# The causal mask of layer 1's attention, moved from selects on the probabilities to matmuls on the scores

## Chip, core and metric

The kernel runs on one core of a Trainium2 chip. The metric is the device time of one execution in microseconds, median of three runs. Engines are named as in the profile: PE (matmuls), PEld (PE's weight loads), DVE, ACT, POOL, and SP, which issues DMAs.

## What is computed

Two transformer layers with a layer norm after each of their four blocks, on x of shape (4, 512, 256). Layer 0 is a grouped-query attention without a mask and a mixture of eight experts. Layer 1, which the change touches, is a causal attention with 16 heads of 16 and a feed-forward block of width 1024:

```python
qkv = x @ W_qkv.T + b_qkv
scores = einsum('bnqd,bnkd->bnqk', q, k) * 0.25
scores = where(triu(ones((S, S)), k=1), -inf, scores)   # key after query
attn = softmax(scores)
out = einsum('bnqk,bnkd->bnqd', attn, v)
y = layernorm(x + out @ W_out.T + b_out)
```

## The kernel before

All code is one program with semaphores written by hand. Each engine walks the same written list of steps, `c_steps` for layer 1, and does its own part of each. The lists are strings (C_START to C_END, lines 82 to 98), so the order on every engine is fixed; an engine that waits holds up all that stands behind it on that engine.

Layer 1's attention goes over 4 batches, 4 groups of 4 heads and 4 key tiles of 128: 64 steps, 16 in a batch. Step k has two parts:

- `cattS` k: PE computes the scores of four heads, transposed (keys on partitions, queries along the row), one PSUM bank each, columns from `P * kt` to 512, so 512, 384, 256 or 128 columns as kt goes from 0 to 3 (L847). Only the first 128 of them, the diagonal block, need a mask. The row maxima have been put into the product as two more rows of q and k, so ACT only takes the exponential (L1003), two heads per instruction. PE signals `s_full` after each pair of heads, ACT `exp_done` after each pair.
- `cattP` k: PE multiplies the probabilities by V and a column of ones (L860), four heads side by side in the 32-column groups of the array.

Between the two stands POOL: after both exponentials it zeroes, with one `affine_select` over the diagonal blocks of four heads (128x512), the probabilities whose key comes after the query (L1436), and signals `masked`. PE waits for `masked` ahead of `cattP` (L858).

`attention_order` (line 119) interleaves: `cattS` k+1, then the fills of step k, then `cattP` k. The fills are the other work of the layer: for the next batch the projections (cX, cQ, cK, cV), the row maxima (m) and the packing of the maxima (cM); for the batch before the normalisation of the heads (cF, cG), the output projection with its layer norm (cP, cN) and the feed-forward (cH, cD). A fill of kind m is a unit of 512 columns: PE computes scores (L824) and adds the causal mask to the diagonal block by a matmul of the identity with `negmask` (L826), DVE reduces it to maxima (L1335). Units go through three PSUM banks in a ring (`take`, `filled`, `consumed`); `negmask` is -1e30 above the diagonal, in bf16. L599 is the helper of all PE transposes, L607 that of all other products of the fills. L1049 to L1070 are DVE's layer norm, L1309 to L1311 its split of q and k into bf16 parts (cK), L993 is ACT's part of cQ and waits for the store of parts two units back; L1007 evacuates the attention output.

POOL's other work in this stage is the gather of layer 0's expert rows for the next batch (L1414), issued when DVE has finished with the batch before. Layer 0's attention has the same two parts (`attS` L641, `attP` L655) with no mask: `attP` waits for `exp_done` of the first pair at its first head and for that of the second pair at its third.

Of the kernel before, what the change touches and what calls it, by code (L numbers as in the profile page):

```python
# [25 lines left out]
ALU = mybir.AluOpType  # L26
# [3 lines left out]
P = 128  # L30
B = 4
# [3 lines left out]
NT = S // P  # L35
# [115 lines left out]
def post_ln_layers(nc, ins, out):  # L151
# [4 lines left out]
    with ExitStack() as ctx:  # L156
# [101 lines left out]
        base = place([E])  # L258
# [104 lines left out]
        s_stack2 = [sem(f"last_q_stacks_loaded{i}") for i in range(2)]  # L363
        s_full = [sem(f"scores_full{i}") for i in range(2)]
        exp_done = [sem(f"exp_done{i}") for i in range(2)]
        masked = sem("probs_masked")
        pv_done = sem("pv_done")
        o_evac = sem("o_evacuated")
        x1_ready = sem("x1_ready")
# [223 lines left out]
        def _(pe):  # L593
# [185 lines left out]
            for step in c_steps:  # L779
# [5 lines left out]
                elif n == "Wb":  # L785
                    transposes(step, [(0, n_b[0:4 + NK, :], ident[0:4 + NK, 0:4 + NK], P)])
                elif n == "Wu":
                    pe.wait_ge(deq, 1)
                    c, half = i // 2, i % 2
                    transposes(step, [(P * r, n_up[:, 4 * half + r, cols(c)], ident, P) for r in range(4)])  # L790
                elif n == "Wul":
                    c, half = i // 2, i % 2
                    consumed(pe, ("Wat", 0, 0))
                    products(step, [((P, 0, 512), [(ua_t[0:RANK, cols(c)], n_ub[0:RANK, 512 * half:512 * half + 512])])])
                elif n == "Wd":
                    pe.wait_ge(deq, 2)
                    transposes(step, [(P * (2 * r + c), n_dn[:, c, cols(2 * i + r)], ident, P)
                                for r in range(2) for c in range(2)])
                elif n == "Wdl":
                    consumed(pe, ("Wat", 0, 2))  # L800
                    products(step, [((P, C * r, C * (r + 1)), [(da_t[0:RANK, cols(2 * i + r)], n_db[0:RANK, :])])
                                    for r in range(2)])
                elif n in ("cX", "cN"):
                    pe.wait_ge(x2_ready if n == "cX" else x3_ready, 2 * b + i + 1)
                    transposes(step, [(P * (2 * t + c), x_sb[:, NT * b + 2 * i + t, cols(c)], ident, P)
                                for t in range(2) for c in range(2)])
                elif n == "cQ":
                    consumed(pe, ("cX", b, 0))
                    consumed(pe, ("cX", b, 1))
                    w_cols = cols(2 * (i % 2) + i // 2)  # L810
                    products(step, [((P, 0, S), [(w1_qkv[:, c, w_cols], c_x_t[:, c, :]) for c in range(2)])])
                elif n == "cV":
                    products(step, [((P, C * t, C * (t + 1)),
                                     [(c_x_t[:, c, cols(2 * i + t)], w1_qkv[:, c, 2 * C:3 * C]) for c in range(2)])
                                    for t in range(2)])
                elif n == "max":

                    qt, h0, nh = MAXES[i]
                    if i % (len(MAXES) // 2) == 0:
                        pe.wait_ge(cs_stack[h0 // (NH // 2)][b % 2], 32 * (b // 2 + 1))  # L820
                    dst = take(pe, step)
                    w = P * (qt + 1)
                    for g in range(nh):
                        nc.tensor.matmul(dst[:, w * g:w * (g + 1)], cq_stack[0:STACK, b % 2, h0 + g, cols(qt)],  # L824
                                         ck_stack[0:STACK, b % 2, h0 + g, 0:w], start=True, stop=True)
                        last = nc.tensor.matmul(dst[:, w * g + P * qt:w * (g + 1)], identb, negmask,  # L826
                                                start=False, stop=True, skip_group_check=True)
                    last.then_inc(full_of(step), 1)
                elif n == "cM":
                    pe.wait_ge(m_parts, b + 1)  # L830
                    dst = take(pe, step).bitcast(BF16)
                    for t in range(NT):
                        last = nc.tensor.transpose(dst[0:2 * NH, cols(t)], mparts[:, t, :, :].rearrange("p a h -> p (a h)"),
                                                   identb)
                    last.then_inc(full_of(step), 1)
                elif n == "cattS":
                    hg, kt = i // NT, i % NT
                    k = head0 * B + headc * b + i
                    if i == 0:
                        pe.wait_ge(s_m, 32 * (b + 1))  # L840
                        pe.wait_ge(kones, 1)
                    for g in range(4):
                        h = 4 * hg + g
                        if g % 2 == 0:

                            pe.wait_ge(exp_done[g // 2], k)
                        last = nc.tensor.matmul(ps[:, g, P * kt:S], ck_stack[0:STACK + 2, b % 2, h, cols(kt)],  # L847
                                                cq_stack[0:STACK + 2, b % 2, h, P * kt:S], start=True, stop=True)
                        if g % 2:
                            last.then_inc(s_full[g // 2], 1)  # L850
                elif n == "cattP":
                    hg, kt = i // NT, i % NT
                    if i == 0:
                        consumed(pe, ("cV", b, 0))
                        consumed(pe, ("cV", b, 1))
                    if kt == 0:
                        pe.wait_ge(o_evac, HG * (B + b) + hg)
                    pe.wait_ge(masked, headc * b + i + 1)  # L858
                    for g in range(4):
                        last = nc.tensor.matmul(ps[32 * g:32 * g + 32, 4, P * kt:S],  # L860
                                                cv_aug[:, b % 2, kt, 4 * hg + g, :],
                                                cprobs[:, i % 2, g, P * kt:S], start=(kt == 0), stop=(kt == NT - 1))
                    last.then_inc(pv_done, 1)
                elif n == "cF":
                    pe.wait_ge(o_evac, HG * (B + b + 1))
                    transposes(step, [(P * hg, co_sb[:, hg, cols(i)], ident, P) for hg in range(HG)])
                elif n == "cG":
                    consumed(pe, ("cF", b, 2 * i))
                    consumed(pe, ("cF", b, 2 * i + 1))
                    transposes(step, [(P * (2 * t + c), cattn[:, t, cols(c)], ident, P)  # L870
                                for t in range(2) for c in range(2)])
                elif n == "cP":
                    consumed(pe, ("cG", b, i))
                    products(step, [((P, C * t, C * (t + 1)),
                                     [(c_a_t[:, c, cols(2 * i + t)], w1_o[:, c, :]) for c in range(2)])
                                    for t in range(2)])
                elif n == "cH":
                    consumed(pe, ("cN", b, 0))
                    consumed(pe, ("cN", b, 1))
                    products(step, [((P, 0, S), [(w_up[:, c, cols(i)], c_x3_t[:, c, :]) for c in range(2)])])  # L880
                elif n == "cI":

                    half, k = i // NK, i % NK
                    consumed(pe, ("cN", b, half))
                    tok = slice(C * half, C * half + C)
                    products(step, [((P, 0, C), [(w_up[:, c, cols(k)], c_x3_t[:, c, tok]) for c in range(2)])])
                elif n == "cD":
                    for k in range(NK):
                        consumed(pe, ("cI", b, NK * (i // 2) + k) if ("cI", b, 0) in unit_no else ("cH", b, k))
                    products(step, [((P, 0, C), [(hid_t[:, k, cols(i)], w_dn[:, k, :]) for k in range(NK)])])  # L890
# [485 lines left out]
        def _(pool):  # L1376
# [47 lines left out]
            for step in c_steps:  # L1424
                n, b, i = step
                if n == "cL" and i == 1 and b + 1 < B:
                    pool.wait_ge(x2_ready, 2 * b + 2)
                    gather(b + 1)
                elif n == "cattS":

                    k = head0 * B + headc * b + i
                    kt = i % NT
                    pool.wait_ge(exp_done[0], k + 1)
                    pool.wait_ge(exp_done[1], k + 1)
                    diag = cprobs[:, i % 2, :, P * kt:P * (kt + 1)]
                    nc.gpsimd.affine_select(out=diag, in_=diag, compare_op=ALU.is_ge, fill=0.0, base=0,  # L1436
                                            pattern=[[0, 4], [1, P]], channel_multiplier=-1).then_inc(masked, 1)


_NAMES = {  # L1440
# [53 lines left out]
```

## Time and profile before

| | before |
|---|---|
| median of 3 runs | 959.66 us (957.38 to 961.69) |
| the profiled execution, own time | 959.16 us |
| its span, first to last instruction | 957.4 us |
| granted TensorE clock, mean | 0.921 |
| PE busy | 815.9 us (85%), 4084 instructions |
| DVE busy | 466.6 us (49%) |
| ACT busy | 372.8 us (39%) |
| POOL busy | 131.3 us (14%), 129 instructions |

Layer 1's attention fills the stretch from 600 to 906 us of the span. The granted clock has two values in this trace, 1.00 (2.4 GHz) and 0.50 (1.2 GHz), so a mean between them tells how much of a stretch ran at either. PE's busy time counts a matmul to its modelled end, and matmuls overlap: the true interval of a matmul in a stream is the distance from its start to the next start.

### The profile page before, as it was taken

What the parts mean: (1) busy time and instruction counts of PE and PEld (TensorE: products, weight loads), DVE (VectorE), ACT (ScalarE), POOL (GpSimd) and SP (SyncE); (2) the same over time, 40 slices, a digit from 0 to 9 for tenths busy, and PEclk for the clock granted to TensorE, in tenths of its full rate; (3) what the DMA queues carried; (4) which work ended last, traced back from release to release, by engine and by line L of the source; (5) the groups of instructions that cost most, each with busy time, mean ns of one, the idle gap of its engine ahead of it and who ended that gap; (6) DMA issues with size and microseconds to landing.
All of it is one profiled execution on the core that took longest, in us unless ns stands there. A gap on an engine that the chain in (4) does not pass through costs nothing. (4 is left out here: it accounts for less than half of the span.)

```text
span 957.4 us, 12102 instructions
## 1 busy us (share of the span) xinstructions
PE 815.9 (85%) x4084; PEld 438.9 (46%) x4085; DVE 466.6 (49%) x1317; ACT 372.8 (39%) x591; POOL 131.3 (14%) x129
## 2 busy tenths in 40 slices
PE   4598999999998649999983687979798979979986
PEld 3223435444345336666642334435354544543675
DVE  3721741751436222222246877587745675553263
ACT  3387685875742001111121121644332533246230
POOL 0000000000000611111665010213010100112000
PEclk8699999999999979999975787989899979999989
DMA  6558116025060051111110854002800180000000
GB/s 191 112 168 173 60 61 130 0 64 83 23 219 23 1 162 45 46 47 44 33 55 22 253 161 136 2 2 65 222 1 2 34 253 1 2 1 23 12 12 22
DMA packets 55259, 71.01 MB, mean 74 GB/s; under 512 B 8678, under 2 KB 49592, under 8 KB 53672
## 3 DMA queue, kind: packets, MB, share of 16 engines
q1 hardware_dynamic: 52824, 65.22, 24.8%
q0 software_dynamic: 2384, 5.12, 2.0%
q8 instruction: 30, 0.49, 0.2%
q14 instruction: 21, 0.17, 0.1%
HBM read 46.45 MB, written 23.74 MB: 73 GB/s over the span
## 5 line engine op out<-in xcount | busy, mean ns | idle before, releaser
L607 PE MATMUL ps<-arena 128*128 128x256 f32 (+5 forms) x1084 | 335.6, 459 | 16.2 <-ACT arena L980 4.3
L607 PEld LDWEIGHTS ps<-arena 128*128 128x128 f32 (+1 forms) x1084 | 203.8, 198 | 107.4 <-issue 67.7
L922 ACT ACTIVATE arena<-ps 128x1024 f32<-128x1024 f32 x128 | 124.0, 1026 | 40.8 <-PE ps L641 40.7
L599 PE MATMUL ps<-arena 128*128 128x128 f32 (+4 forms) x430 | 71.6, 311 | 74.5 <-DVE arena L1070 32.2
L1335 DVE TENSOR_REDUCE arena<-ps 128x1 f32<-128x512 f32 (+3 forms) x176 | 101.2, 636 | 43.4 <-PE ps L826 42.6
L1003 ACT ACTIVATE arena<-ps 128x1024 f32<-128x1024 f32 (+3 forms) x128 | 83.3, 705 | 86.4 <-PE ps L847 86.1
L599 PEld LDWEIGHTS ps<-arena 128*128 128x128 f32 (+4 forms) x430 | 56.4, 158 | 97.2 <-DVE arena L1070 36.0
L722 PE MATMUL ps<-arena 128*128 x184 | 86.6, 593 | 1.2 <-DVE arena L1239 1.2
L1436 POOL TENSOR_SCALAR_AFFINE_SELECT arena<-arena 128x512 f32<-128x512 f32 x64 | 43.2, 675 | 288.2 <-ACT arena L1003 288.1
L641 PE MATMUL ps<-arena 96*128 96x512 bf16 x256 | 71.9, 394 | 12.6 <-DMA arena<-parts_dram 9.8
L824 PE MATMUL ps<-arena 96*128 96x128 bf16 (+3 forms) x256 | 65.5, 315 | 11.6 <-DVE arena L1335 7.0
L655 PE MATMUL ps<-arena 128*32 128x512 f32 x512 | 70.2, 616 | 0.0
L947 ACT ACTIVATE arena<-ps 128x512 f32<-128x512 f32 x23 | 13.8, 598 | 143.0 <-PE ps L722 143.0
L847 PE MATMUL ps<-arena 98*128 98x512 bf16 (+3 forms) x256 | 50.1, 316 | 11.3 <-ACT arena L1003 8.2
L1382 POOL DMA_INDIRECT id_dram<-arena x16 | 15.7, 979 | 316.1 <-DVE arena L1221 311.5
L641 PEld LDWEIGHTS ps<-arena 96*128 96x128 bf16 x256 | 18.4, 98 | 88.4 <-ACT arena L922 34.6
L826 PE MATMUL ps<-arena 128*128 128x128 bf16 x256 | 50.6, 227 | 0.0
L860 PE MATMUL ps<-arena 128*32 128x128 f32 (+3 forms) x512 | 48.9, 454 | 0.0
L824 PEld LDWEIGHTS ps<-arena 96*128 96x128 bf16 x256 | 25.5, 100 | 43.7 <-DVE arena L1335 27.4
L722 PEld LDWEIGHTS ps<-arena 128*128 128x128 f32 x184 | 33.1, 190 | 25.3 <-issue 24.2
L739 PE MATMUL ps<-arena 128*128 x184 | 43.6, 380 | 0.8 <-ACT arena L953 0.8
L847 PEld LDWEIGHTS ps<-arena 98*128 98x128 bf16 x256 | 18.5, 99 | 55.8 <-issue 31.0
(135 smaller groups left out, 757.0 us busy)
## 6 DMA issues: line engine op xcount, KB each, us to landing
arena<-stacks_dram SPq DMA_DIRECT2D x16, 768.0 KB, 6.6
arena<-in_gate_up_proj SPq DMA_DIRECT2D x8, 1024.0 KB, 8.8
arena<-parts_dram SPq DMA_DIRECT2D x48, 128.0 KB, 4.3
stacks_dram<-arena SPq DMA_DIRECT2D x16, 384.0 KB, 3.0
arena<-in_down_proj SPq DMA_DIRECT2D x8, 512.0 KB, 9.3
stacks_dram<-arena SPq DMA_DIRECT2D x16, 256.0 KB, 3.2
parts_dram<-arena SPq DMA_DIRECT2D x8, 384.0 KB, 4.2
yg_dram<-arena SPq DMA_DIRECT2D x23, 128.0 KB, 1.7
```

Of the source, the lines that this page charges most:

```text
L599: last = nc.tensor.transpose(dst[0:rows, col:col + n], src, idn)
L607: last = nc.tensor.matmul(dst[0:rows, lo:hi], a, w, start=(n == 0), stop=(n == len(pairs) - 1))
L641: last = nc.tensor.matmul(ps[:, g, :], k_stack[0:STACK, b % 2, hg, cols(kt)], q_stack[0:STACK, b % 2, 4 * hg + g, :], start=True, stop=True)
L655: last = nc.tensor.matmul(ps[32 * g:32 * g + 32, 4, :], v_aug[:, kt, hg, :], (probs0, probs1)[i % 2][:, g, :], start=(kt == 0), stop=(kt = ...
L722: last = nc.tensor.matmul(ps[:, 2 * half + up, :], xg_t[:, half, c, :], gu[:, e, c, FE * up:FE * (up + 1)], start=(c == 0), stop=(c == 1))
L824: nc.tensor.matmul(dst[:, w * g:w * (g + 1)], cq_stack[0:STACK, b % 2, h0 + g, cols(qt)], ck_stack[0:STACK, b % 2, h0 + g, 0:w], start=Tru ...
L826: last = nc.tensor.matmul(dst[:, w * g + P * qt:w * (g + 1)], identb, negmask, start=False, stop=True, skip_group_check=True)
L847: last = nc.tensor.matmul(ps[:, g, P * kt:S], ck_stack[0:STACK + 2, b % 2, h, cols(kt)], cq_stack[0:STACK + 2, b % 2, h, P * kt:S], start= ...
L860: last = nc.tensor.matmul(ps[32 * g:32 * g + 32, 4, P * kt:S], cv_aug[:, b % 2, kt, 4 * hg + g, :], cprobs[:, i % 2, g, P * kt:S], start=( ...
L922: nc.scalar.activation(probs[:, 2 * p:2 * p + 2, :], ps[:, 2 * p:2 * p + 2, :], ACT.Exp)\
L1003: nc.scalar.activation(cprobs[:, i % 2, 2 * p:2 * p + 2, P * kt:S], ps[:, 2 * p:2 * p + 2, P * kt:S], ACT.Exp).then_inc(exp_done[p], 1)
L1335: nc.vector.tensor_reduce(mneg[:, qt, h0:h0 + nh], filled(v, step)[:, 0:nh * w].rearrange("p (h n) -> p h n", n=w), AX.X, ALU.max, negate= ...
```

## The change

Each `cattS` issues four more matmuls, two after each pair of score matmuls: `negmask` as the stationary operand and the identity as the moving one, so that -1e30 is added to the scores whose key comes after the query, in the diagonal 128 columns of each head's bank. They stand ahead of the signal `s_full`. POOL's 64 selects and their semaphore go, and `cattP` waits for ACT's `exp_done`, the first pair ahead of its first head and the second pair ahead of its third.

```diff
--- before.py
+++ after.py
@@ -363,7 +363,6 @@
-        masked = sem("probs_masked")
@@ -847,6 +846,9 @@
                         last = nc.tensor.matmul(ps[:, g, P * kt:S], ck_stack[0:STACK + 2, b % 2, h, cols(kt)],
                                                 cq_stack[0:STACK + 2, b % 2, h, P * kt:S], start=True, stop=True)
                         if g % 2:
+                            for d in (g - 1, g):
+                                last = nc.tensor.matmul(ps[:, d, cols(kt)], negmask, identb, start=False, stop=True,
+                                                        skip_group_check=True)
                             last.then_inc(s_full[g // 2], 1)
@@ -855,8 +857,9 @@
                     if kt == 0:
                         pe.wait_ge(o_evac, HG * (B + b) + hg)
-                    pe.wait_ge(masked, headc * b + i + 1)
                     for g in range(4):
+                        if g % 2 == 0:
+                            pe.wait_ge(exp_done[g // 2], head0 * B + headc * b + i + 1)
                         last = nc.tensor.matmul(ps[32 * g:32 * g + 32, 4, P * kt:S],
@@ -1426,15 +1429,6 @@
                 if n == "cL" and i == 1 and b + 1 < B:
                     pool.wait_ge(x2_ready, 2 * b + 2)
                     gather(b + 1)
-                elif n == "cattS":
-
-                    k = head0 * B + headc * b + i
-                    kt = i % NT
-                    pool.wait_ge(exp_done[0], k + 1)
-                    pool.wait_ge(exp_done[1], k + 1)
-                    diag = cprobs[:, i % 2, :, P * kt:P * (kt + 1)]
-                    nc.gpsimd.affine_select(out=diag, in_=diag, compare_op=ALU.is_ge, fill=0.0, base=0,
-                                            pattern=[[0, 4], [1, P]], channel_multiplier=-1).then_inc(masked, 1)
```

## Rows read from the trace of the kernel before

**Rows 1.** The page: busy time, share of the span and instructions of each engine.

```profile
PE 815.9 (85%) x4084; PEld 438.9 (46%) x4085; DVE 466.6 (49%) x1317; ACT 372.8 (39%) x591; POOL 131.3 (14%) x129
```

**Rows 2.** Busy us by engine, count, granted clock: attention's end; a half-clock stretch.

```profile
864.00:905.70 41.70, 41.23 (x224) 22.19 (x222) 11.40 (x45) 18.79 (x31) 6.84 (x10) 0.99 0.06 20
639.20:646.00 6.80, 5.40 (x24) 2.69 (x25) 6.11 (x28) 3.84 (x5) 0.64 (x1) 0.50 0.01 3
```

**Rows 3.** Who waited for whom, 560 to 957 us: total, times, longest.

```profile
POOL arena L1436 <- ACT arena L1003: 288.1, 60, 43.1
...
PEld ps L860 <- issue: 23.3, 59, 0.8
...
PEld ps L860 <- POOL arena L1436: 1.5, 2, 0.8
```

**Rows 4.** Timeline around the P parts of steps 25 and 1: start, duration, engine.

```profile
697.04 0.63 POOL L1436 TENSOR_SCALAR_AFFINE_SELECT arena<-arena 128x512 f32<-128x512 f32 x1 [8.29 <-ACT arena L1003]
...
705.36 0.22 PE L826 MATMUL ps<-arena 128*128 128x128 bf16 x1
...
705.50 0.16 PEld L860 LDWEIGHTS ps<-arena 128*32 128x32 f32 x8 [0.27 <-issue]
...
600.95 0.64 POOL L1436 TENSOR_SCALAR_AFFINE_SELECT arena<-arena 128x512 f32<-128x512 f32 x1 [0.76 <-ACT arena L1003]
...
601.37 0.61 PE L847 MATMUL ps<-arena 98*128 98x256 bf16 x4
...
601.90 0.16 PEld L860 LDWEIGHTS ps<-arena 128*32 128x32 f32 x8 [0.21 <-issue]
```

**Rows 5.** Timeline: a P part and what follows it, layer 0 and layer 1.

```profile
150.97 1.06 PE L655 MATMUL ps<-arena 128*32 128x512 f32 x8
151.97 1.04 PE L641 MATMUL ps<-arena 96*128 96x512 bf16 x4
...
600.37 1.07 PE L860 MATMUL ps<-arena 128*32 128x512 f32 x8
```

**Rows 6.** Timeline of PE: first and last of eight matmuls of 128 columns.

```profile
599.81 0.22 PE L824 MATMUL ps<-arena 96*128 96x128 bf16 x1
...
600.22 0.22 PE L826 MATMUL ps<-arena 128*128 128x128 bf16 x1
```

**Rows 7.** Timeline: stalls of PE and ACT, with idle time before and releaser.

```profile
636.81 0.34 PE L833 MATMUL ps<-arena 128*32 128x128 bf16 x3 [0.82 <-DVE arena L1343]
...
640.60 1.89 PE L847 MATMUL ps<-arena 98*128 98x512 bf16 x4 [2.96 <-DMA arena<-arena]
...
672.64 1.26 ACT L993 ACTIVATE arena<-ps,arena 128x512 f32<-128x512 f32 x2 [6.32 <-DMA stacks_dram<-arena]
...
674.45 0.29 PE L847 MATMUL ps<-arena 98*128 98x128 bf16 x2 [2.71 <-ACT arena L1003]
...
743.08 0.50 PE L847 MATMUL ps<-arena 98*128 98x384 bf16 x2 [0.42 <-ACT arena L1003]
...
860.89 1.12 PE L599 MATMUL ps<-arena 128*128 128x128 f32 x4 [4.18 <-DVE arena L1070]
```

**Rows 8.** Waits of PE for cV on DVE, 640 to 700 us.

```profile
PE ps L599 <- DVE arena L1321: 1.3, 1, 1.3
```

**Rows 9.** Timeline: DVE operations beside a select of POOL, and the same without.

```profile
655.13 0.64 POOL L1436 TENSOR_SCALAR_AFFINE_SELECT arena<-arena 128x512 f32<-128x512 f32 x1 [2.22 <-ACT arena L1003]
...
655.21 0.83 DVE L1310 CAST arena<-arena 128x512 bf16<-128x512 f32 x1
...
669.42 0.43 DVE L1310 CAST arena<-arena 128x512 bf16<-128x512 f32 x1
...
853.43 0.16 DVE L1068 SCALAR_TENSOR_TENSOR arena<-arena 128x2 f32<-128x2 f32 x1
...
854.01 0.64 DVE L1068 SCALAR_TENSOR_TENSOR arena<-arena 128x2 f32<-128x2 f32 x1
```

**Rows 10.** Groups of DVE instructions, 600 to 906 us: count, busy us, mean ns.

```profile
L1310 DVE CAST arena<-arena 128x512 bf16<-128x512 f32 x8 | 5.2, 645 | 0.3
```

## The prediction

> **What bounds the kernel now.** I read the page first. PE is busy for 85% of the span, every other engine for less than half [rows 1], so work added to PE is suspect and work taken from POOL is not yet a gain. Then the table by stage. In the last 42 us of layer 1's attention PE is busy 41.23 of 41.70 us [rows 2]: nothing there can hide PE work. Then the waits. POOL's selects wait 288 us for ACT, so POOL is idle nearly all the time, and PE's weight loads of the P part wait for POOL only twice, 1.5 us in all [rows 3]. Last the timeline of single steps, to see whether even that is real. In step 25 the select starts at 697.04 and the P part at 705.50: it was ready 7.8 us early, because the fills stand between S k+1 and P k. The P part starts 0.14 us after the last matmul ahead of it. The tightest case is step 1, which has no fills: the select ends at 601.59 (600.95 + 0.64); the four score matmuls of 256 columns start at 601.37 and last to 601.98 by the model, and the weights of P load at 601.90, as they do elsewhere just ahead of the running matmul's modelled end [rows 4]. So POOL holds PE up nowhere that I can find. What ends the attention stage is PE's own stream, broken by a few waits for DVE, ACT and DMA at the seams of the batches [rows 7].
>
> **The change, part by part.**
>
> *Four matmuls per S part.* 4 x 64 = 256 matmuls of 128 columns in bf16, each with its own weight load. The maxima have the same kind: score and mask matmuls by turns, new weights each time. Eight of them start from 599.81 to 600.22, so 0.41/7 = 0.0586 us each at the full clock; the weight loads are hidden [rows 6]. 256 x 0.0586 = 15.0 us. The steps whose S part lies at the half clock pay double. I count two, steps 16 and 17: at 640.60 four score matmuls of 512 columns take 1.89 us [rows 7] in a stretch whose granted clock is 0.50, the lower level of 1.2 GHz [rows 2]. That is 8 x 0.0586 = 0.5 us more. Sum 15.5 us, 0.234 us for each S part.
>
> The Trainium skill, TensorE: Matmul & The Clock Gate, section Back-to-back issue gap, speaks against the change more strongly: it gives about 81 ns for a 128-column matmul in a stream of weight loads and matmuls. By that figure the four mask matmuls would cost an estimated 20.7 us instead of 15.0. The rows at hand measure the very pattern, so the sum goes by them.
>
> *What of it is covered.* An added matmul costs nothing where PE then waits for something whose start does not depend on it. I walked the 64 steps:
> - Ahead of the packing of maxima PE waits 0.82 us for DVE L1343, which hangs on the last max unit, issued earlier [rows 7]. The S part in between is covered, in three batches: 0.7 us.
> - In batches 1 and 2 ACT sits 6.32 us on the DMA of the q and k parts, then PE 2.71 us on ACT, and then 1.3 us on DVE's cV [rows 7, 8]. Two S parts ahead of the stall and one inside it are covered, twice: 6 x 0.234 = 1.4 us.
> - In the last batch PE waits 4.18 us for a layer norm [rows 7]; two S parts lie in the shadow of that chain: 0.5 us.
> - Where the fills are few, PE waits inside the S part for the exponentials of the step before, as the 0.42 us at 743.08 [rows 7]. There the first pair's masks are covered, some seven times, 0.12 to 0.23 us each: 1.3 us.
> - The first steps of batches 1 and 2 wait in the chain of transposes and head normalisation: 0.6 us.
>
> Together 4.5 us. In the bursts of maxima PE also waits for DVE in a ring, but DVE itself idles at each seam between two bursts while PE does P and S, so a later PE makes DVE later too: I count no cover there. Nor in steps 53 to 63 [rows 2]. If none of this cover held, the cost would be 15.5; if the rings covered too (about 16 more steps), 11.0 - 3.7 = 7.3.
>
> *s_full comes later* by 0.12 us for each pair, and ACT's exponentials with it. P k stands behind S k+1, which already waits for the exponentials of k, so no new wait arises in P; in the steps without fills the delay is that of the fourth point.
>
> *The wait of P.* It moves from `masked` to two `exp_done`. Both are met when S k+1 has started. Saving: nothing with fills between; at most the 1.5 us of [rows 3]. I take 0. Cost of the second wait: layer 0's P part has it and lasts 1.00 us from its start to the next S part (150.97 to 151.97), the same as layer 1's (600.37 to 601.37) [rows 5, 4]. I take 0.
>
> *64 selects go.* POOL is idle otherwise; what stands behind them in its queue, the gather for a later batch, is needed many steps later. Gain 0 on POOL, but not on DVE: the CAST of cK at 655.21, beside a select, took 0.83 us, the same at 669.42 took 0.43; an operation of the layer norm at 854.01 took 0.64 against 0.16 [rows 9]. Eleven DVE operations are stretched so, by 3.8 us in all, operation by operation; nearly half of that is CAST, whose mean of 0.645 over eight is 0.217 above 0.43 [rows 10]. Most lies where PE does not wait. On a chain that PE waits for I find 0.31 and 0.37 us in batch 1, 0.31, 0.31 and 0.31 in batch 2 and 0.48 in batch 3: 2.1 us gained. Bounds: 0 and 3.8. The Trainium skill, SBUF — State Buffer, section Who interferes with whom, says that a DVE instruction with two SBUF inputs and a GpSimd instruction that reads SBUF exclude each other. Its whole promise is this term, and the trace agrees for 854.01.
>
> **The sum.** 15.5 - 4.5 - 2.1 = +8.9 us on the profiled execution's 959.16 (span 957.4 and 1.8 around it): 968.1. The median of the runs is 0.5 higher, so I forecast 968.5 us.
>
> **The rivals.** About 0.5% (4.8 us) is what a measurement of this kernel can tell from no change.
>
> *Full price.* The cover is not there, or more S parts fall to the lower clock: a stall that moves can bring another stretch like that of 639.2 to 646.0 [rows 2], in which 6.8 us do the work of 3.4. Then 15.5 - 0 to 2, plus 3.4: +13 to +19, about 975. For it: PE is the bound nearly throughout. Against: the stalls of [rows 7] are real idle time. By the skill's 81 ns the sum would be an estimated 5.7 us above the forecast, in this rival's range. Chance 0.17.
>
> *Nearly hidden.* The rings cover (7.3 us left, as above), and DVE gains its full 3.8: +3.5, about 963. A low-clock stretch that vanishes because the stalls ahead of it shrink brings it near, 8.9 - 3.4 = +5.5. Against: DVE idles at the seams. Chance 0.15.
>
> *Faster.* The handoff over POOL is the wait after all. Its place is the idle time ahead of L860's weight loads, 23.3 us over 59 steps, which the profile puts down to "issue" [rows 3]; a semaphore that arrives late could hide in it. Removed, the sum is 8.9 - 23.3 = -14.4, about 945; the change wins from the point at which over 8.9 us of it are POOL's. Against: in step 25 the select was long done and the 0.27 us were there still [rows 4]. Chance 0.06.
>
> **The numbers.** Forecast 0.62, full price 0.17, nearly hidden 0.15, faster 0.06. Slower by over 0.5%: the first two, less a tail of the forecast, 0.77. Within 0.5%: 0.17. Faster: 0.06. The range runs from 962.0, which takes in part of the nearly hidden case, to 975.5, all cover gone (959.66 + 15.5 = 975.2).
>
> **What would show it.** Right: no row L1436; 256 more matmuls that start 0.058 us apart within L847's groups; P parts still 0.14 us behind the matmul ahead; steps 53 to 63 longer by 2.6 us (11 x 0.234); the waits of 4.18 and 2.71 us shorter by about 0.5 each; CAST back at 0.43. Wrong: P parts that follow faster than before (POOL was the wait), mask matmuls at over 0.07 us, or other low-clock stretches than before.

## The result and the profile after

| | before | after |
|---|---|---|
| median, first series | 959.38 us (4 runs) | 972.22 us (4 runs) |
| ratio, 95% interval | | 1.0128 [1.0111, 1.0146] |
| profiled execution, own time | 959.16 us | 973.52 us |
| its span | 957.4 us | 971.7 us |
| first S part | 596.38 us | 602.28 us |
| last P part | 904.80 us | 922.14 us |

The changed kernel is slower, by 12.8 us in this series. It was run in two more series, beside the kernel before: 1.0086 [1.0064, 1.0107] and 1.0091 [1.0060, 1.0122] (below). So the change costs 8 to 12 us by the three ratios, 6 to 14 with their intervals; the forecast was +8.9. Two executions of later series that took far longer, 4387 us of the kernel before and 1647 us of the one with the masks ahead of the scores, are in no ratio.

The page of the changed kernel, busy time by engine, answers to [rows 1]:

```profile
PE 832.3 (86%) x4340; PEld 454.9 (47%) x4341; DVE 464.1 (48%) x1317; ACT 374.3 (39%) x591; POOL 88.2 (9%) x65
```

PE has 256 instructions more, POOL 64 fewer. POOL lost 43 us of work and DVE 2.5 us, PE gained 16.4.

The attention stage by itself, from the first S part to the last P part, and its end, from the P part of step 53 to that of step 63; first the kernel before, then the changed one (columns as in [rows 2]):

```profile
596.38:904.80 308.42, 274.46 (x1669) 145.66 (x1668) 180.96 (x498) 126.46 (x202) 46.94 (x68) 0.95 0.17 48
868.08:904.80 36.72, 36.72 (x205) 20.27 (x204) 7.34 (x27) 16.61 (x27) 6.20 (x9) 1.00 0.05 16
```

```profile
602.28:922.14 319.86, 290.59 (x1925) 162.11 (x1924) 177.22 (x498) 127.81 (x202) 3.79 (x4) 0.95 0.16 46
883.04:922.14 39.10, 39.10 (x241) 22.32 (x240) 6.32 (x23) 16.62 (x27) 0.00 (x0) 1.00 0.04 15
```

The stage grew by 11.4 us. Its end, where PE never idles in either kernel, grew by 2.38 us with 36 matmuls more: nine S parts at 0.26 us.

The other 2.9 us of the two spans' difference lie outside the attention stage, where the code of both kernels is the same. Ahead of the attention the changed kernel's profile lies 5.9 us back, behind it 3.0 us forward. The same window of the expert stage, untouched by the change, first before, then after (the granted clock is the third number from the end):

```profile
290.00:390.00 100.00, 75.97 (x287) 48.39 (x285) 30.83 (x91) 13.47 (x22) 25.15 (x26) 0.91 0.21 59
```

```profile
290.00:390.00 100.00, 75.16 (x263) 46.90 (x262) 29.86 (x95) 12.38 (x20) 24.25 (x25) 0.85 0.19 55
```

One ran at 0.91, the other at 0.85, and got 24 matmuls less done. In further profiles of the two kernels the first S part stood at 598.2 (before), 597.9 and 599.2 us (after): most of the 5.9 us is the chance of one execution. What follows the last P part took 52.6 and 49.6 us in two profiles of the kernel before, 49.6, 49.6 and 51.1 in three of the changed one.

Now the S part in steps 24 to 26 of the changed kernel, from PE's timeline; the P part is L863, the scores L846, the masks L850:

```profile
712.58 0.22 PE L825 MATMUL ps<-arena 128*128 128x128 bf16 x1
...
712.73 1.06 PE L863 MATMUL ps<-arena 128*32 128x512 f32 x8
713.73 0.39 PE L846 MATMUL ps<-arena 98*128 98x256 bf16 x2
713.96 0.28 PE L850 MATMUL ps<-arena 128*128 128x128 bf16 x2
714.07 0.38 PE L846 MATMUL ps<-arena 98*128 98x256 bf16 x2
714.29 0.28 PE L850 MATMUL ps<-arena 128*128 128x128 bf16 x2
714.41 0.33 PE L823 MATMUL ps<-arena 96*128 96x384 bf16 x1
...
715.07 0.22 PE L825 MATMUL ps<-arena 128*128 128x128 bf16 x1
715.22 0.16 PEld L863 LDWEIGHTS ps<-arena 128*32 128x32 f32 x8 [0.27 <-ACT arena L1006]
```

A pair of masks goes from 713.96 to 714.07, 0.11 us; over whole intervals (below) four of them cost 0.23 us, 0.057 a matmul. The P part of step 25 still loads its weights 0.15 us after the last fill (715.07 to 715.22) with the same 0.27 us of idle time ahead of it as in [rows 4]. Over all steps those idle times, 23.3 us in [rows 3], are what they were:

```profile
PEld ps L863 <- issue: 23.1, 57, 1.0
```

The 1.5 us that [rows 3] puts down to POOL are now 0.3 us put down to ACT. They had held up no P part: at both places, 653.08 and 804.27, PE was busy with matmuls of a fill up to its start.

And DVE's CAST of cK, [rows 10], is at its undisturbed time:

```profile
L1313 DVE CAST arena<-arena 128x512 bf16<-128x512 f32 x8 | 3.4, 426 | 0.3
```

The most telling comparison is one that the rows allow without a model: how much longer is the interval from each P part to the next than it was before? Interval k runs from P k-1 to P k and holds the S part of step k+1. Of 63 intervals, 29 grew by 0.22 or 0.23 us, 17 by 0.28, eleven by no more than 0.11 or not at all, and six moved otherwise (the interval in brackets): -1.35 (22), -0.68 (38), -0.76 (52), +0.42 (15), +0.97 (47), +1.10 (53).

### The profile page after: what moved, and what is told of

The parts are those of the page before. It is cut to its first block and busy times, and to the rows that moved or that the text cites. A ratio compares the mean times of both kernels' runs of the same rounds, so it can differ in the third digit from the quotient of the medians.

```text
span 971.7 us, 12485 instructions
## 1 busy us (share of the span) xinstructions
PE 832.3 (86%) x4340; PEld 454.9 (47%) x4341; DVE 464.1 (48%) x1317; ACT 374.3 (39%) x591; POOL 88.2 (9%) x65
## 5 line engine op out<-in xcount | busy, mean ns | idle before, releaser
L598 PE MATMUL ps<-arena 128*128 128x128 f32 (+4 forms) x430 | 69.6, 305 | 73.6 <-DVE arena L1073 32.2
L1338 DVE TENSOR_REDUCE arena<-ps 128x1 f32<-128x512 f32 (+3 forms) x176 | 101.2, 634 | 50.2 <-PE ps L825 49.6
L721 PE MATMUL ps<-arena 128*128 x184 | 89.4, 611 | 1.2 <-DVE arena L1242 1.2
L640 PE MATMUL ps<-arena 96*128 96x512 bf16 x256 | 71.9, 394 | 12.3 <-DMA arena<-parts_dram 9.5
L846 PE MATMUL ps<-arena 98*128 98x512 bf16 (+3 forms) x256 | 56.5, 313 | 10.0 <-ACT arena L1006 6.2
L863 PE MATMUL ps<-arena 128*32 128x128 f32 (+3 forms) x512 | 48.9, 454 | 0.0
L721 PEld LDWEIGHTS ps<-arena 128*128 128x128 f32 x184 | 34.2, 196 | 27.1 <-issue 26.0
L738 PE MATMUL ps<-arena 128*128 x184 | 43.6, 380 | 0.8 <-ACT arena L956 0.8
L738 PEld LDWEIGHTS ps<-arena 128*128 128x128 f32 x184 | 34.9, 190 | 15.1 <-issue 11.6
L1367 DVE TENSOR_TENSOR arena<-ps,arena 128x256 f32<-128x256 f32 x16 | 6.8, 424 | 72.3 <-PE ps L606 72.2
```

Of the source, the lines that this page charges most:

```text
L598: last = nc.tensor.transpose(dst[0:rows, col:col + n], src, idn)
L640: last = nc.tensor.matmul(ps[:, g, :], k_stack[0:STACK, b % 2, hg, cols(kt)], q_stack[0:STACK, b % 2, 4 * hg + g, :], start=True, stop=True)
L721: last = nc.tensor.matmul(ps[:, 2 * half + up, :], xg_t[:, half, c, :], gu[:, e, c, FE * up:FE * (up + 1)], start=(c == 0), stop=(c == 1))
L738: last = nc.tensor.matmul(ps[:, 6 + half, 0:C], hh_t[:, half, f, :], dn[:, e, f, :], start=(f == 0), stop=(f == NF - 1))
L1338: nc.vector.tensor_reduce(mneg[:, qt, h0:h0 + nh], filled(v, step)[:, 0:nh * w].rearrange("p (h n) -> p h n", n=w), AX.X, ALU.max, negate= ...
```

## The experiments

### Masks by PE and selects by POOL, and neither

```diff
# e1_masks_and_selects, against the kernel before
                         if g % 2:
+                            for d in (g - 1, g):
+                                last = nc.tensor.matmul(ps[:, d, cols(kt)], negmask, identb, start=False, stop=True,
+                                                        skip_group_check=True)
                             last.then_inc(s_full[g // 2], 1)
```

> The kernel before with the 256 mask matmuls added to the S parts, and POOL's 64 selects, their signal and P's wait for it kept (the selects then zero what is zero already). My theory (matmuls cost PE time, selects only slow DVE): like the changed kernel plus the 2 us that its DVE gains, so 974 us, +15 on before; the stretched CASTs of L1310 stay at a mean of 0.645 us. Rival 'the handoff over POOL was the wait': the gain of the changed kernel is missing here, so it should be far above it, 985 or more. Rival 'the selects cost nothing': equal to the changed kernel, 972.

```diff
# e2_no_mask_at_all, against the changed kernel
-                            for d in (g - 1, g):
-                                last = nc.tensor.matmul(ps[:, d, cols(kt)], negmask, identb, start=False, stop=True,
-                                                        skip_group_check=True)
```

> The changed kernel without its mask matmuls: no causal mask on the probabilities of layer 1's attention at all, neither by PE nor by POOL, P waits for the exponentials. My theory: before less the DVE gain, 957.3 us (-2.1, bounds 0 and -3.8). Rival 'handoff over POOL': 23 us less, 936. With the changed kernel at 972.2 the matmuls would then cost 15 us net of cover; if only the 12.8 of the result, the selects cost nothing and this run is at 959.4.

Measured: e1 970.99 us, 1.0111 [1.0089, 1.0133]; e2 957.64 us, 0.9967 [0.9951, 0.9984], both on 961.07 us for the kernel before. Taking POOL and its handoff out brings 0.3%, not the 2.4% of the rival, and the masks with POOL still in the way cost what they cost without it. The handoff was not the wait. The 974 us, +15, that I expected of e1 were a miss: it is 9.9 us above the kernel before, and its ratio lies among the three of the changed kernel. So the times of e1 don't show what the selects cost.

The intervals show a gain, but not its size. e2 against before: -0.37 in interval 22, -0.13 in 38, -0.46 in 52, nothing elsewhere but where a half-clock stretch moved. The changed kernel against e1, in the same three: -0.34, -0.23, -0.35. That would be 0.9 to 1.0 us on PE's path, where I had 2.1. But half-clock stretches lie in intervals 22 and 38 too, and in the unchanged kernel's repetition (next section) these moved by -0.42 and +0.85 by themselves; only interval 52 stood still there, at +0.01. So only its 0.35 to 0.46 us, against the 0.48 of the forecast, can be read from the profiles. The time of e2 says more: by its ratio 3.2 us, 1.5 to 4.7, under the kernel before. Part of that is the clock: the mean granted clock was 0.925 in its 12 runs and 0.923 in the 23 beside them, about 3.6 us less at 1.2 GHz, an estimate from the spans, worth up to 1.8 us. A gain of 1 and one of 2.1 us both fit. The CAST group of e1, then of e2:

```profile
L1313 DVE CAST arena<-arena 128x512 bf16<-128x512 f32 x8 | 5.2, 650 | 0.3
```

```profile
L1310 DVE CAST arena<-arena 128x512 bf16<-128x512 f32 x8 | 3.4, 427 | 0.3
```

The select stretches it; the masks on PE do not. The Trainium skill, SBUF — State Buffer, section Who interferes with whom, names a DVE cast in a two-port mode, besides an instruction with two SBUF inputs, as one that contends with GpSimd. The stretched CAST fits that, but no run here shows in which mode it was. What a blocked instruction is worth only the chain behind it tells.

### The kernel before once more

> The kernel before, unchanged, as one more kernel: how far two equal kernels stand apart, and a second profile of it. Expected: 959.4 us within 2 us. In the profiled execution of the changed kernel 5.9 us were lost ahead of the attention and 3 us won behind it; if that is the chance of the clock's low stretches, then the start of the first S part (596.4 us before, 602.3 after) lies elsewhere again in this profile, anywhere from 594 to 603; if it is the kernels' own, it is at 596.4 within 0.5.

959.79 us, 0.9994 [0.9981, 1.0007]. Its first S part is at 598.20 us and its attention stage lasts 310.06 us, against 596.38 and 308.42 in the first profile; 50 of the 63 intervals agree to 0.01 us, and the other 13 move with the half-clock stretches, by up to 0.85 us (-0.42 in 22, +0.59 in 23, +0.85 in 38). So one profile's intervals can be read to hundredths where no such stretch is near, its stage to about 2 us.

### The masks ahead of the scores

```diff
                     for g in range(4):
...
+                        if g % 2 == 0:
+                            for d in (g, g + 1):
+                                nc.tensor.matmul(ps[:, d, cols(kt)], negmask, identb, start=True, stop=True)
                         last = nc.tensor.matmul(ps[:, g, P * kt:S], ck_stack[0:STACK + 2, b % 2, h, cols(kt)],
-                                                cq_stack[0:STACK + 2, b % 2, h, P * kt:S], start=True, stop=True)
+                                                cq_stack[0:STACK + 2, b % 2, h, P * kt:S], start=False, stop=True,
+                                                skip_group_check=True)
                         if g % 2:
-                            for d in (g - 1, g):
-                                last = nc.tensor.matmul(ps[:, d, cols(kt)], negmask, identb, start=False, stop=True,
-                                                        skip_group_check=True)
                             last.then_inc(s_full[g // 2], 1)
```

> The changed kernel with the two mask matmuls of each pair of heads issued ahead of the pair's score matmuls (the mask starts the group, the scores are added to it). In the profile of the changed kernel an f32 matmul of the fills starts 0.05 us later where it follows a mask matmul of 128 columns, in some 18 of 64 steps. Theory 'its weight load of 0.19 us isn't covered by a 0.06 us matmul': with the long score matmul last again this goes, -0.9 us on the changed kernel, 971.3, and the distance from the last matmul of the S part to the next f32 one is back at that of before. Rival 'it is the switch from bf16 to f32 itself or a matter of the signal': no change, 972.2.

> The mask matmuls ahead of the score matmuls once more, this time beside the changed kernel on one chip. By the profile's spacing it saves 18 x 0.05 = 0.9 us; the time should be 0.1% under the changed kernel's, which these rounds may just not resolve. If it is over 1 us slower, the spacing misleads.

970.70 us, 1.0104 [1.0082, 1.0127], and beside the changed kernel 969.24 against 970.41 us. The time does not resolve it. The intervals do: all 17 that had grown by 0.28 us are at 0.23, in both profiles. From the last matmul group of the S part through four f32 matmuls to P, first the changed kernel, then this one:

```profile
894.37 0.28 PE L850 MATMUL ps<-arena 128*128 128x128 bf16 x2
894.48 1.93 PE L606 MATMUL ps<-arena 128*128 128x512 f32 x4
896.35 0.85 PE L863 MATMUL ps<-arena 128*32 128x384 f32 x8
```

```profile
890.81 0.38 PE L849 MATMUL ps<-arena 98*128 98x256 bf16 x2
891.03 1.88 PE L606 MATMUL ps<-arena 128*128 128x512 f32 x4
892.84 0.85 PE L864 MATMUL ps<-arena 128*32 128x384 f32 x8
```

1.87 us from the first f32 matmul to P in the one, 1.81 in the other. The switch from bf16 to f32 is still there, so it is not that; what changed is the matmul ahead. An f32 weight load takes 0.19 us, and a matmul of 0.057 us ahead of it doesn't give enough cover. Intervals 54 and 62 fit: there the last score matmul ahead of the f32 ones has 128 columns in the kernel before too, and they paid 0.23 only. That is 17 x 0.05 = 0.85 us of the change's cost that the sum did not have.

### The masks twice

```diff
-                            for d in (g - 1, g):
+                            for d in (g - 1, g, g - 1, g):
```

> The changed kernel with each pair's two mask matmuls issued twice (-2e30 instead of -1e30, the same probabilities): 256 more matmuls of 128 columns, nothing else. Theory 'PE's stream is the bound and most of the cover is spent': gross 256 x 0.058 = 14.9 us; what the seams still cover, at most the 3 to 4 us that the first 256 got, goes off: +11 to +14.5 on the changed kernel run beside it, the interval from one P part to the next longer by 0.23 us wherever it already was, 0.05 of f32 weight loads not paid again. Rival 'the first 256 cost something of their own, a wait or the fetch of instructions, and the matmuls are cheap': under +8.

> The changed kernel, unchanged, beside the other two on one chip, with a second profile. Expected 972 us within 2; the attention stage, from the first S part to the last P part, at 319.9 us within 1 whatever happens ahead of it (5.9 us lost there in its first profile, 1.5 to 3.5 in those of its relatives). If it comes out near 971, the two masked kernels measured before (971.0 and 970.7) are no faster than it, and the 0.9 us of the order of matmuls can't be seen in the time.

979.33 us, 1.0191 [1.0163, 1.0218]; the changed kernel beside it 968.93 us, 1.0086 [1.0064, 1.0107]. So the second 256 matmuls cost 10.4 us, the first 7.1 by the medians of this series (961.86 before). That misses the 11 to 14.5 that I had named, by a little, and is above the rival's 8. The changed kernel's 968.93 misses its 972 within 2 as well. The intervals are as expected: 0.45 where there was 0.23, 0.51 where there was 0.28, 0.00 still in 4, 14, 30 and 46. What I had not put in is the clock. The attention stage of this kernel, then of the changed one beside it:

```profile
599.90:925.62 325.72, 297.96 (x2180) 173.12 (x2180) 177.15 (x498) 128.28 (x202) 3.78 (x4) 0.98 0.16 46
```

```profile
597.85:914.44 316.59, 286.86 (x1924) 160.62 (x1924) 177.13 (x498) 127.42 (x202) 3.78 (x4) 0.97 0.16 47
```

A granted clock of 0.98 means that 14 us of the stage ran at 1.2 GHz; 0.97 here, and 0.95 in the first profiles, mean 21 and 32 to 33. The changed kernel's stage came out at 319.9, 316.6 and 318.8 us in three profiles, in step with its granted clock of 0.95, 0.97 and 0.96. The expectation of 319.9 within 1 was wrong.

### Masks only where they are covered, and only where they are not

```diff
# e7_masks_where_covered, against the kernel before; POOL's select skips the same steps, where P waits for exp_done
+BY_PE = (3, 5, 15, 17, 18, 23, 31, 33, 39, 47, 49, 53)
...
+                            if headc * b + i in BY_PE:
+                                for d in (g - 1, g):
+                                    last = nc.tensor.matmul(ps[:, d, cols(kt)], negmask, identb, start=False, stop=True,
+                                                            skip_group_check=True)
```

> The kernel before, with the mask by PE in the 12 steps whose interval from P part to P part did not grow by more than 0.06 us in the changed kernel (3, 5, 15, 17, 18, 23, 31, 33, 39, 47, 49, 53) and POOL's select in the other 52. Theory of cover: these 12 cost nothing, and a few stretched DVE operations go: the attention stage 0 to 0.7 us shorter than before's 308.4 to 310.1, the time 959.8, no difference that can be measured. Rival 'cover is an illusion, each S part costs its 0.23 us somewhere later': +2.8 us, the stage at 311 to 313.

961.45 us, 1.0000 [0.9983, 1.0017] on 961.86. The stage of this kernel:

```profile
598.52:906.82 308.30, 275.75 (x1718) 148.48 (x1717) 180.59 (x498) 126.72 (x202) 38.57 (x56) 0.95 0.16 48
```

49 matmuls more in the record (48 and one that the other trace lacks), and 308.30 us against 308.42 before, both at a clock of 0.95. By the ratio's interval a cost of 2.8 us is excluded. The twelve are nearly free: against before, intervals 2, 4, 17 and 23 grew by 0.11, 0.11, 0.06 and 0.11 us, and no other by more than 0.01; 22 and 38, where half-clock stretches lie, fell by 0.20 and 0.33. Why step 15's are, in the rows of this kernel's PE around it (masks L853, wait for the packed maxima L834):

```profile
637.98 0.28 PE L848 MATMUL ps<-arena 98*128 98x128 bf16 x2
638.10 0.28 PE L853 MATMUL ps<-arena 128*128 128x128 bf16 x2
638.21 0.28 PE L848 MATMUL ps<-arena 98*128 98x128 bf16 x2
638.33 0.28 PE L853 MATMUL ps<-arena 128*128 128x128 bf16 x2
639.19 0.34 PE L834 MATMUL ps<-arena 128*32 128x128 bf16 x3 [0.59 <-DVE arena L1352]
```

The wait that was 0.82 us in [rows 7] is 0.59: the four masks were done inside it.

```diff
# e10_masks_only_where_paid, against the changed kernel
+LEFT_OUT = (3, 5, 15, 17, 18, 23, 31, 33, 39, 47, 49, 53)
...
-                            for d in (g - 1, g):
+                            for d in (g - 1, g) if headc * b + i not in LEFT_OUT else ():
```

> The changed kernel with the masks left out in the 12 steps whose interval didn't grow (3, 5, 15, 17, 18, 23, 31, 33, 39, 47, 49, 53), so that those steps have no causal mask. Theory of cover: the 208 matmuls of the other 52 carry the whole cost; the attention stage stays within 0.7 us of the changed kernel's in the same series. Rival 'all 256 pay alike': 12 x 0.23 = 2.8 us shorter.

> The changed kernel once more, since its first two series gave ratios of 1.0128 and 1.0086 with intervals that don't touch. If the truth is one number and the series scatter with the chip and the hour: between the two, 1.009 to 1.012. The attention stage 316.5 to 320 us, and in step 47's interval about 1 us more than before with a landing of 3.8 us for a row of maxima.

970.58 us, 1.0092 [1.0060, 1.0125], beside the changed kernel's 970.41 us, 1.0091 [1.0060, 1.0122]: as if the 208 matmuls of the other steps carried the whole cost, but with intervals of 3 us to either side the times alone don't exclude the rival's 2.8 us. The stage lasted 322.35 us against 318.82, outside the 0.7 that I had named, at a clock of 0.94 against 0.96. Interval by interval the left-out masks bring at most 0.15 us each and 0.4 together in 2, 4 and 17, where the clock was the same in both. So the cover rests on e7 and on the intervals.

## Why the prediction came out as it did

**Right in sign and mechanism, 8.9 us forecast; the three ratios, on 959.4 us, give 12.3, 8.3 and 8.7.** By its own steps:

- *Gross price, 15.5 us.* The matmuls cost 0.0575 us each, 14.7 in all, plus 0.3 to 0.9 at the half clock: 6 to 16 of the masks started there in the three profiles, among them those of interval 15 in the first, which paid 0.42. I had counted two S parts there; in the profile before, steps 0, 39 and 54 start at the half clock too. The 0.0586 from the maxima held; the 81 ns of the Trainium skill, TensorE: Matmul & The Clock Gate, section Back-to-back issue gap, did not. Missing were 0.85 us of f32 weight loads that lost their cover (masks first).
- *Cover, 4.5 us.* The places were right in the main: ahead of the packing of maxima (intervals 14, 30, 46), at the handoffs to ACT (2, 4, 32, 48) and in the first steps of batches 1 and 2 (16, 17, 33). Against 0.23 each, these ten kept back 2.3 us; I had 2.6 for them, with seven handoffs. The wait of 0.42 us at 743.08 in [rows 7] is 0.30 in the changed kernel:

```profile
753.85 0.50 PE L846 MATMUL ps<-arena 98*128 98x384 bf16 x2 [0.30 <-ACT arena L1006]
```

  What the stalls on DMA and cV (22, 38) cover can't be told from the clock there: in the three profiles of the changed kernel interval 38 moved by -0.68, -2.27 and -0.50 us. In the last batch the wait was another than I had said. The 4.18 us of [rows 7] did not shrink; a wait ahead of it, 0.94 us, was gone: the masks and the shorter layer norm ahead took it up. Before, then after:

```profile
856.05 0.65 PE L599 MATMUL ps<-arena 128*128 128x128 f32 x4 [0.94 <-DVE arena L1070]
```

```profile
869.92 0.66 PE L598 MATMUL ps<-arena 128*128 128x128 f32 x4
...
874.75 1.11 PE L598 MATMUL ps<-arena 128*128 128x128 f32 x4 [4.18 <-DVE arena L1073]
```

  The rings of the maxima cover nothing, as said: intervals 5 to 13 and 25 to 29 paid 0.22 or 0.23 each. e7 shows the cover in the time, e10 in the intervals.
- *DVE gain, 2.1 us.* The sign is shown, the size is open. DVE's busy time in the stage fell from 180.96 to 177.22 us, the 3.8 that I had as the bound; what of it reaches PE is the question. In batch 3 interval 52 gives 0.35 to 0.46 where I had 0.48. In batches 1 and 2 the profiles give 0.37 and 0.13 where I had 0.68 and 0.93, which looks too high, but the kernel before repeated moved the same intervals by as much; the time of e2, -3.2 us with up to 1.8 of it from the clock, leaves 2.1 possible.
- *P's wait, 0.* Right: 23.3 us of idle time before, 23.1 after, and e2 rules out the rival "faster": it gained 3.2 us, not 23.
- *Ahead and behind.* The first series' profile took 5.9 us ahead of the attention and gave 3.0 back behind it, at other clocks; a forecast of the change can't hold these. With them gone the stage says +11.4, of which 0.97 in interval 47 and 1.10 in interval 53 are named below, 0.23 of each being the masks' own. The three stages of the changed kernel and the two of the kernel before differ by 9.2 us in the mean.

That 8.9 lies so near 8.3 and 8.7 is in part luck. The sum had neither the 0.85 us of weight loads nor the late landing of interval 47, up to 0.9 us, and it did not have what worked the other way, less time at 1.2 GHz. In the two series that gave 8.3 and 8.7 the mean granted clock of the changed kernel's runs was 0.931 and 0.929, that of the kernel before 0.923 and 0.926: about 15 and 3 us less at the low clock, an estimate from the spans, each worth up to half. In the first series, the one with 12.3, the changed kernel's runs had 0.926.

"Full price" (+13 to +19) is above two of the three ratios with their intervals; the first one's interval, 10.7 to 14.0 us, reaches into it. What speaks against it is e7, which shows the cover, and the stage's mean of +9.2. "Nearly hidden" (+3.5 to +5.5) needs rings that cover; they don't.

No version here that keeps the whole mask beats the kernel before. e2, which has none, shows what could be won with masks that cost nothing: about 0.3%.

## What to carry to other kernels

Work moved from an idle engine to the one that bounds the kernel costs its full issue time wherever that engine's stream is dense, however short the instructions are; here 0.057 us a matmul, and 46 of the 63 intervals paid at least 0.22 us for their four. Before such a move, ask whether anyone waited for the idle engine: compare when it was done with when its result was used (7.8 us apart in step 25), not the length of its waits. To tell a change of 1% from the chance of one execution, compare the intervals between the same instruction's occurrences in both traces: 50 of 63 agreed to 0.01 us in one kernel run twice, and the ones that don't name the place. Profile the unchanged kernel twice first: its own intervals moved by up to 0.85 us where half-clock stretches lie.

## What the runs showed that I had not expected

**A small DMA landed late with a fetch of instructions beside it.** Interval 47 grew by 0.97 us, 0.74 beyond the masks, because S 48 waited for the rows of maxima. First PE's row, then the queues between 847 and 854 us, all of the changed kernel:

```profile
853.04 0.60 PE L846 MATMUL ps<-arena 98*128 98x512 bf16 x2 [0.68 <-DMA arena<-arena]
```

```profile
q1 hardware_dynamic: 64, 0.03, 2.0%
q8 instruction: 1, 0.02, 1.2%
```

The one packet of instructions stands beside the 64 of the maxima; their landing took up to 3.8 us there and 2.1 to 2.2 in the kernel before. In all twelve profiles it is the same: in six (the changed kernel's three, e1, e4 and e9) such a packet, of 16 KB, overlaps the transfer, and the landing took 3.2 to 3.9 us; in the other six (the kernel before twice, e2, e5, e7 and e10) none does, and it took at most 2.4. Interval 47 grew beyond the masks' own share only in the first six, by 0.45 (e8) to 1.17 us (e6) in all; it grew by 0.23 in e10 and, with the masks twice, by 0.45 in e5. No run moved that packet alone, so that it is the cause is likely, not shown.

**With more matmuls, mostly less time at the low clock.** In the attention stage 33 to 42 us ran at 1.2 GHz without masks on PE (before, its repetition, e2), 21 to 32 in three profiles of the changed kernel, 14 with the masks twice. The runs point the same way: a mean granted clock of 0.923 to 0.926 in the series of the kernel before, 0.926 to 0.931 in those of the changed one, 0.934 with the masks twice. But e10, with 208 of the 256 masks, had 42 us there in its profile and 0.926 in its runs, no better than before; so this is a tendency, and no run shows its cause. Each microsecond there costs up to half of itself. In the kernel before, the stretches at 639.2 and 857.6 us begin inside the stalls of 2.96 and 4.18 us of [rows 7], that at 676.7 us 2.3 us behind the stall of 2.71, and the masks shorten some stalls: 2.71 us ahead of S 23 in [rows 7], 1.94 in the changed kernel. But the changed kernel's 1.10 us in interval 53 are the opposite case: the same stall of 4.18 us lies ahead of it in both, and after it PE's dense work met more of the low stretch (873 to 880 us) than before (858 to 864).
